# A graph layer and an LSTM on one core: the exact LSTM steps written out instead of looped

## The reference

```python
def step(carry, xp):                 # xp: the gates of the input, already projected
    h, c = carry
    gates = xp + h @ W_hh.T
    i, f, g, o = jnp.split(gates, 4, axis=-1)
    c = sigmoid(f) * c + sigmoid(i) * tanh(g)
    h = sigmoid(o) * tanh(c)
    return ((h, c), h)
_, hs = jax.lax.scan(step, (h0, c0), x_proj)   # 6250 steps, 256 features
```

## Time and profile before

| | us |
|---|---|
| three timed runs, median | 2264.18 |
| lowest and highest of them | 2255.17, 2269.06 |
| profiled execution, span from its first to its last instruction | 2255.1 |
| exact steps before the While (copies of L1676, steps 33 to 40) | 1655.12 to 1687.43 |
| first and second pass of the While | 1687.43 to 1914.02, and on to about 2142 |

### The profile page before, as it was taken

The page is one execution under the profiler, slowest core; times in us unless marked ns, Lnnn a source line. Parts: engine busy times, 40 slices in busy tenths (PEclk is TensorE's granted clock), DMA queues, the critical chain, the costliest instruction groups (busy, mean ns, idle before and its releaser), DMA issues.

```text
span 2255.1 us, 43532 instructions
## 1 busy us (share of the span) xinstructions
PE 1974.7 (88%) x13354; PEld 1571.9 (70%) x13354; DVE 1599.4 (71%) x4208; ACT 1174.6 (52%) x3147; POOL 166.0 (7%) x224
## 2 busy tenths in 40 slices
PE   5678989999999999999989989996679888898845
PEld 4567876666666666666668878885478887888734
DVE  8876888777777777777727767777866665666696
ACT  4564435555455555545523346667865554555526
POOL 3342001000000000000000000000000000000070
PEclk8799998999999999999999999997579999999975
DMA  4322320101001010010133212223543333233303
GB/s 119 100 68 74 97 95 23 33 23 30 28 23 33 26 32 24 26 33 23 33 121 93 69 47 117 109 109 136 163 128 98 113 117 109 92 117 112 107 0 114
DMA packets 96300, 169.81 MB, mean 75 GB/s; under 512 B 7773, under 2 KB 68401, under 8 KB 95944
## 3 DMA queue, kind: packets, MB, share of 16 engines
q1 hardware_dynamic: 67413, 86.80, 11.8%
q10 hardware_dynamic: 27088, 77.11, 10.9%
q0 software_dynamic: 1744, 5.21, 0.8%
HBM read 110.53 MB, written 58.56 MB: 75 GB/s over the span
## 4 chain that ended last, share of the span: by engine, by line
PE 52%; DVE 24%; ACT 10%; issue 7%; DMA 4%; ACTq 1%; DVEq 0%; POOL 0%; SPq 0%; POOLq 0%
PE psum L632 27%; PE psum L627 7%; PE psum L785 7%; PE psum L742 4%; DVE scr L1686 2%; ACT scr L1087 2%; DVE scr L1684 2%; DVE wp L1575 2%; DVE scr L1477 2%; ACT scr L1095 2%; DVE bufB L1603 1%; DVE scr L1682 1%; PE psum L820 1%; DMA out_dram<-wq 1%; ACT scr L1054 1%
## 5 line engine op out<-in xcount | busy, mean ns | idle before, releaser
L632 PE MATMUL psum<-halves,counts 128*128 128x512 f32 x2401 | 759.7, 423 | 16.2 <-ACT counts L992 16.2
L1502 DVE TENSOR_TENSOR wx<-rs_buf 128x392 bf16<-128x392 bf16 (+1 forms) x1568 | 545.1, 390 | 212.0 <-PE psum L627 208.2
L992 ACT ACTIVATE counts<-psum 128x392 fp32r<-128x392 f32 x784 | 390.3, 498 | 358.9 <-PE psum L627 357.6
L785 PE MATMUL psum<-bufB,wx 128*128 (+1 forms) x3392 | 425.5, 283 | 49.8 <-DVE bufB L1688 42.3
L785 PEld LDWEIGHTS psum<-bufB,wx 128*128 128x128 f32 x3392 | 399.0, 193 | 76.2 <-issue 61.1
L632 PEld LDWEIGHTS psum<-halves,counts 128*128 128x128 f32 x2401 | 393.6, 189 | 65.9 <-ACT counts L992 21.8
L627 PEld LDWEIGHTS psum<-wx 128*128 128x128 bf16 x3136 | 170.7, 99 | 198.9 <-issue 192.2
L627 PE MATMUL psum<-wx 128*128 128x98 bf16 x3136 | 284.8, 212 | 3.9 <-DVE wx L1502 2.8
L742 PE MATMUL psum<-bufA,wx 128*128 (+1 forms) x800 | 180.0, 376 | 3.1 <-POOL rs_buf L493 3.1
L742 PEld LDWEIGHTS psum<-bufA,wx 128*128 128x128 f32 x800 | 146.7, 188 | 20.1 <-issue 3.3
L1095 ACT ACTIVATE scr<-scr 128x125 f32<-128x125 f32 x280 | 86.1, 307 | 126.5 <-DVE scr L1686 121.4
(11 more groups left out here) (261 smaller groups left out, 2503.3 us busy)
## 6 DMA issues: line engine op xcount, KB each, us to landing
bufA<-gates_of_x ACTq DMA_DIRECT2D x136, 500.0 KB, 3.4
gates_of_x<-bufB SPq DMA_DIRECT2D x24, 1000.0 KB, 3.9
x_times_eps_plus_sums<-scr SPq DMA_DIRECT2D x50, 128.0 KB, 1.7
sums_by_feature<-scr SPq DMA_DIRECT2D x50, 128.0 KB, 1.9
scr<-x_times_eps_plus_sums SPq DMA_DIRECT2D x49, 128.0 KB, 2.1
wx<-in_x_dram SPq DMA_DIRECT2D x25, 250.0 KB
x_plus_mix<-wx SPq DMA_DIRECT2D x25, 250.0 KB, 4.8
bufB<-x_plus_mix SPq DMA_DIRECT2D x25, 250.0 KB, 2.7
```

The lines of the kernel that those rows point to most:

```text
L632: return mm(psum[:, 3 + v, :], cnt[v][:, hi, :], xhl[:, hi, :, :].rearrange("p s d -> p (s d)"), start=(hi == 0), stop=(hi == NT - 1))
L785: return mm(gate_half(u, m, gate), whhv[:, k, (2 * gate + m) * P:(2 * gate + m + 1) * P], h, start=False, stop=(k == 1), skip_group_check= ...
L992: fn(cnt[v][:, :, c * u:c * (u + 1)], psum[:, CB[u % 4], 0:PER * KEYS].rearrange("p (c h) -> p h c", h=NT), ACT.Copy).then_inc(S["c_sb"], 1)
L1502: last = tt(to, tab2[:, 0:k_, :].unsqueeze(1).broadcast_to([P, PER // 2, k_, 2]), keysT[v][:, part_, g0:g0 + PER // 2, :].unsqueeze(2).bro ...
```

## The change

All loops over exact steps are replaced by Python loops, so that each engine has these steps one after another in its list, with fixed places in `hs`. In the first sweep, where the base is a number, the semaphore values become fixed too; in the `While` they are still computed from its register. The `While` and the loops over the short steps stay. The work of a step and its order are the same.

```diff
             def time_step(done, t, u):
-                h = [hs[:, ds(t, 1), c, :].rearrange("p t j -> p (t j)") for c in range(2)]
+                h = [hs[:, t, c, :] for c in range(2)]
...
             def up_to_cut(base):          # TensorE
-                with pe.Fori(1, CUT // 2) as i:
-                    for u in range(2):
-                        time_step(pe.snap(base + 2 * i + u), 2 * i + u, u)
+                for t in range(2, CUT):
+                    time_step(base + t if isinstance(base, int) else pe.snap(base + t), t, t % 2)
...
-            with pe.Fori(SHORT // 2, CUT // 2) as i:
-                for u in range(2):
-                    time_step(pe.snap(2 * i + u), 2 * i + u, u)
+            for t in range(SHORT, CUT):
+                time_step(t, t, t % 2)
...
             def up_to_cut(base, before):  # ScalarE
-                with act.Fori(0, CUT // 2 - 1) as i:
-                    for u in (1, 0):
-                        t = 2 * i + 2 - u
-                        done = act.snap(base + t)
-                        fetch(done, t, u)
-                        act.wait_ge(S[f"pre_ld{1 - u}"], 16 * (before + i) + 16)
-                        act.wait_ge(S["hth_act"], 2 * done)
-                        fill(1 - u, loaded[1 - u])
-                        sweep_step(done, u)
-                later_step(base, before, CUT - 1)
+                for t in range(1, CUT):
+                    later_step(base, before, t)
...
-            with act.Fori(SHORT // 2 + 1, CUT // 2) as i:
-                for u in range(2):
-                    exact_step(act.snap(2 * i + u), 2 * i + u, u, i, True)
+            for t in range(SHORT + 2, CUT):
+                exact_step(t, t, t % 2, t // 2, True)
...
             def half_step(done, t, u, m):  # DVE
-                tt(hs[:, ds(t + 1, 1), m, :].rearrange("p t j -> p (t j)"), s_o[:, cut], th[:, cut], ALU.mult).then_inc(S["hh_v"], 1)
+                tt(hs[:, t + 1, m, :], s_o[:, cut], th[:, cut], ALU.mult).then_inc(S["hh_v"], 1)
...
-                with dve.Fori(0, CUT // 2 - 1) as i:
-                    for u in (1, 0):
-                        t = 2 * i + 2 - u
-                        dve.wait_ge(S[f"pre_ld{1 - u}"], 16 * (before + i) + 16)
-                        fill(1 - u, loaded[1 - u])
-                        sweep_step(dve.snap(base + t), t, u)
-                later_step(base, before, CUT - 1)
+                for t in range(1, CUT):
+                    later_step(base, before, t)
...
-            with dve.Fori(SHORT // 2 - 1, CUT // 2 - 1) as i:
-                for u in (1, 0):
-                    t = 2 * i + 2 - u
-                    dve.wait_ge(S[f"pre_ld{1 - u}"], 16 * i + 16)
-                    fill(1 - u, loaded[1 - u])
-                    sweep_step(dve.snap(t), t, u)
-            later_step(0, 0, CUT - 1)
+            for t in range(SHORT - 1, CUT):
+                later_step(0, 0, t)
```

More of the change, by code:

```diff
@@ L1111, in later_step @@
             def later_step(base, before, t):
-                done, u = act.snap(base + t), t % 2
+                done, u = base + t if isinstance(base, int) else act.snap(base + t), t % 2
                 if t < LS - 2:
@@ L1705, in later_step @@
                 fill(1 - u, loaded[1 - u] if t < LS - 1 else kept[0])
-                sweep_step(dve.snap(base + t), t, u)
+                sweep_step(base + t if isinstance(base, int) else dve.snap(base + t), t, u)
             def up_to_cut(base, before):
```

## The result

| | before | after |
|---|---|---|
| median of 4 runs (lowest to highest), us | 2261.92 (2255.17 to 2269.06) | 2244.39 (2243.73 to 2245.93) |
| ratio to before, 95% interval | | 0.9925 (0.9899 to 0.995) |
| profiled execution: span, us | 2255.1 | 2242.8 |
| steps 1 to 39, first and second sweep, us | 168.52, 168.52 | 157.90, 157.92 |
| flag's memset to TensorE's next matmul, back and out, us | 1.66, 1.43 | 5.31, 4.93 |

The changed kernel takes 0.75% less: 17.5 us between the medians, 12.3 us between the two profiled spans.

What follows compares the result with a forecast made beforehand. Looped exact steps were taken to pay 0.57 us a pair, through ScalarE's late loop closing. Savings of 22.0 + 1.4 + 0.3 = 23.7 us less 3.8 for jumps gave 19.9 off 2264.18: 2244.3 us, range 2233 to 2259.

Steps and rivals of the forecast that it cites:

- The sweeps: Steps 1 to 39 of both sweeps in the While: 168.52 us falls to 157.51 each, 22.0 us saved in both.
- The explanation behind it: At each loop closing the chain goes through ScalarE's branch, register work and DMA issue, costing 0.57 us a pair.
- The first pass: Six exact steps, 34 to 39: 0.8 us saved in four steps plus 0.6 estimated beside them, 1.4 us together.
- The loop entries: Register setting at both loops' entries, step 0 to 1: 0.3 us saved, between 0 and 1.1.
- The jump: Top of the While reloaded after each of two passes, body no longer held: 1.9 us each, 3.8 us added.
- Net: Whole kernel: 23.7 us gross less 3.8 us for the jumps, 19.9 us saved.
- A free jump: Rival at the While's jump back: code held or loaded during the check, full 23.7 us saved, 2240.5 us; chance 0.23.
- A dear jump: Rival at the While's jumps: two blocks one after the other, 13.6 us, net 10.1 us saved, 2254 us; chance 0.13.
- A stop at each block: Rival in the written-out steps: each of about 24 new blocks stops its engine, 25.7 us slower, 2290 us; chance 0.07.
- Only the branch goes: Rival in the exact steps: register work stays, so steps keep most of the 0.57 us a pair; chance 0.05.

Runs made afterwards that it cites:

- the straight kernels: Changed kernel with the While's first two passes written straight on, with check between, without it, or also without a While behind: 2240.60, 2230.73, 2230.88 us.
- written_6: Kernel before with six of each sweep's 38 looped steps written out on all three engines: 2254.93 us, one run.
- scalar_vector_tensor_14: Kernel before with all of ScalarE's and DVE's looped exact steps written out, and fourteen of TensorE's in each sweep: 2249.31 us, ratio 0.9945.
- changed_again: The changed kernel run and profiled once more, nothing altered: 2244.10 us, ratio to before 0.9933.
- scalar_vector: Kernel before with ScalarE's and DVE's exact steps written out, TensorE keeping its loop: 2245.49 us, ratio 0.9945.

## Why the prediction was right

It gave 2244 us, 0.9% faster; it is 2244.39 us, 0.75% faster. Most of the sum held, and one term was too small by half.

*The sweeps* (22.0 us, from 4.145 us a step): 21.2 us. The comparison inside one trace, written-out steps beside looped ones, was right to 0.4 us a sweep. That rest is DVE's: in each sweep two steps, at the same places, take 4.31 to 4.33 us (last section). In the straight kernels, which don't have them, a sweep takes 157.53 to 157.56 us, against 157.51 forecast.

*The explanation behind it* was wrong in one point: "at each closing of the loop the chain goes through ScalarE's branch, its register work and its DMA issue". Taking that away alone brings 0.07 us a pair. The row was read rightly, ScalarE is late itself there, but so are DVE and TensorE, and a wait that is seen at one engine says nothing of what stands behind it. The sum wasn't touched by this, because it used the price of the pair as a whole and the change took all three loops away.

*The first pass* (1.4 us): the four steps from 35 to 39 take 16.58 us, 0.8 less, as forecast; of the three intervals beside them, for which 0.6 was estimated, two gave 0.09 and 0.08 us and the third, step 34 to 35, took 0.41 more (6.56 us in place of 6.15; 5.86 in the second profile of the same kernel, so it moves between executions). *The loop entries* (0.3 us): where step 0 to 1 ran at the upper clock it is 5.76 before and 5.64 after, 0.12 us a sweep.

*The jump* is the term that was mis-sized: "I take 1.9 us a jump", 3.8 in both; it is 3.65 us back and 3.44 us out, 7.1 us. That the body would no longer be held, that the second jump is the one that leaves, and that all three engines load at those places were right. The row that it was sized by, a small transfer's landing, is too short. It left 0.9 us for what goes around a block's own 1.0; the branch has 1.0 to 1.5 us of transfer and 2.4 us around it, and TensorE alone stands 3.14 us longer with one block of its own on queue 8 in that stretch. The Trainium skill, "Runtime: NRT & Kernel Launch", section "Instruction fetch mechanics", says that a taken branch to code that isn't held waits for a fetch while straight code hides its own: both agree with the runs (4.80 us with TensorE's body long, 1.67 with it short, 157.53 us for a straight sweep). The same section of the Trainium skill gives TensorE 128 KiB in blocks of 16 KiB, or 64 bytes an instruction. The trace has 68 instructions a step on TensorE (64 matmuls and weight loads, four for waits and registers), so 20 written steps are 85 KiB and 28 are 119, an estimate from that section. The body of 20 (written_6) was held and the one of 28 (scalar_vector_tensor_14) was not; it is inside the 128 KiB by less than one block, and code behind it is fetched ahead as well, so these runs neither confirm nor refute that size.

*Net*, 14.9 us by these sizes (21.2 + 0.6 + 0.2 - 7.1), against 19.9 forecast. The two profiled spans have 12.3: step 0 to 1 took 1.2 us of it by its clock, and 1.5 us went in stretches beside the terms (0.6 up to step 33, 0.2 behind the jump back, 0.7 behind the jump out), less 0.1 that step 40 to 41 gave. The medians have 17.5, and 18.2 in the group of changed_again. The median of before that the forecast started from, 2264.18 us, was 2.3 us above the one that the result is compared with. So the time met to 0.4 us is partly luck: a saving 2.4 us too large, taken off a start 2.3 us too high.

*The rivals.* A free jump: no, though scalar_vector shows that the jump back costs only 0.34 us from step 39 to 41 where ScalarE and DVE alone make it far. A dear jump, 13.6 us: no. A stop at each block: no; queue 8 brought 27 blocks more and the steps stayed at 4.14 to 4.15 us; only DVE's two steps a sweep may be a trace of it, 0.17 us each. (It counts 86 newly written steps; they are 82, which the register operations in the last section bear out.) Only the branch goes: no.

## What to carry to other kernels

Where engines hand a result round a ring, a loop's cost stands on all of them, and taking it from the one that is seen late uncovers the next: of 0.58 us a pair, single engines gave 0.07 to 0.23 and all three the whole. A body that grows beyond what the engine holds pays for its jump at once and in full, some 3.5 us here, so write out few steps or all, and multiply the price by the number of jumps: half of the steps written out came out no better than the loop. If the usual number of passes is known, write those straight on and leave a loop behind for the rest; here that gave 0.8% with the check between the passes kept, and 1.2% without it.

## What the runs showed of the hardware that was not expected

A TensorE operand whose address comes from a register cost 0.085 us a step (4.23 in place of 4.145), loop or not. DVE's wait ahead of its write of the state was 0.48 to 0.51 us in a loop and 0.37 written out, in both halves of both steps of a pair. That speaks for its address and not for the branch, and the kernel before has a register operation of the write's own line in each half of its 82 looped steps, which the changed kernel hasn't; it wasn't tried by itself:

```profile
L1688 DVEq FUSED_REGOPS  x164: 57/67/88, 1657.3 to 2133.2; - x164
```

The time of a far branch was a block's transfer (1.0 to 1.5 us) and 2.4 us beside it, back or ahead; a branch to code that was held took 0.17 to 0.19.

DVE has two steps in each sweep of the changed kernel that take 0.17 us more, and they return in the same steps of both sweeps and in the profile of changed_again. The timeline shows the place, the work behind the first half's write of the state:

```profile
1783.06 0.29 DVE L1677 TENSOR_TENSOR bufB<-scr 128x125 f32<-128x125 f32 x1 [0.37 <-ACT scr L1093]
1783.51 0.29 DVE L1671 TENSOR_TENSOR scr<-scr 128x125 f32<-128x125 f32 x1 [0.16 <-ACT scr L1085]
```

These start 0.45 us apart, elsewhere 0.27; the sigmoid that the row names was done before DVE's write ended (at 1783.29 and 1783.35 us), so the 0.16 us are DVE's own. Two blocks of code came on queue 14 from 1782 to 1785 us; that DVE crosses into a new block there is argued, not shown.
